# A decoder layer on one core: attention scores computed twice, small TensorE tiles, and a new order on every engine

## The reference

```
x = x + attention(layernorm(x))          # 16 heads of 16, causal, W_qkv, W_out
x = x + cross(layernorm(x), context)     # one head over 256 features, key mask
x = x + ffn(layernorm(x))                # 256 -> 2 x 704 -> 256
attention: softmax(Q K^T / 4 + causal) V for each head, then W_out
cross:     softmax(x ctx^T / 16 + mask) ctx
bit_linear(x, w, g): xn = rms_norm(x, g)
                     xq = round(xn * 127/max|xn|), an integer per row times a scale
                     wq = round(w / mean|w|) clipped to -1, 0, 1, times mean|w|
                     xq @ wq.T
ffn:       gate, up = bit_linear(x, gate_w, g1);  h = gate*sigmoid(gate)*up
           bit_linear(h, down_w, g2)
```

## Time and profile before

| | us |
|---|---|
| median of 3 runs (254.17 to 254.43) | 254.26 |
| profiled execution | 254.95 |
| its span, first to last instruction | 253.2 |
| TensorE busy, share of the span | 218.7, 86% |
| VectorE | 215.2, 85% |
| ScalarE | 147.9, 58% |
| GpSimd | 110.7, 44% |
| mean granted TensorE clock, of full | 0.922 |

### The profile page before, as it was taken

The page is one execution under the profiler, slowest core; times in us unless marked ns, Lnnn a source line. Parts: engine busy times, 40 slices in busy tenths (PEclk is TensorE's granted clock), DMA queues, the critical chain, the costliest instruction groups (busy, mean ns, idle before and its releaser), DMA issues. The chain is left out here.

```text
span 253.2 us, 7285 instructions
## 1 busy us (share of the span) xinstructions
PE 218.7 (86%) x2384; PEld 167.2 (66%) x2384; DVE 215.2 (85%) x639; ACT 147.9 (58%) x386; POOL 110.7 (44%) x209
## 2 busy tenths in 40 slices
PE   3867899989899999999999999999999999666433
PEld 3746686758686868686868686868687877442121
DVE  1398948699999999999999999999999989988741
ACT  2024273657685868585858585858585858443231
POOL 7222011337272727272726262727263626464640
PEclk9975999999999999999999999999999999975555
DMA  6993001010101010101010101001010111000000
GB/s 212 377 356 99 0 3 43 4 41 3 45 22 44 23 43 23 45 21 44 21 46 23 43 23 41 25 25 41 27 39 17 50 34 32 1 25 0 21 21 21
DMA packets 11108, 12.81 MB, mean 51 GB/s; under 512 B 1025, under 2 KB 10305, under 8 KB 11073
## 3 DMA queue, kind: packets, MB, share of 16 engines
q1 hardware_dynamic: 11008, 12.36, 15.0%
q0 software_dynamic: 64, 0.00, 0.0%
HBM read 10.26 MB, written 2.10 MB: 49 GB/s over the span
## 5 line engine op out<-in xcount | busy, mean ns | idle before, releaser
L1348 POOL TENSOR_TENSOR zh<-hh,gd 128x352 f32<-128x352 f32 x16 | 15.2, 947 | 54.4 <-DVE hh L1025 54.4
L320 PE MATMUL bankU<-yaT,wqkv 128*128 128x128 f32 x256 | 35.2, 295 | 0.8 <-ACT yaT L627 0.6
L320 PEld LDWEIGHTS bankU<-yaT,wqkv 128*128 128x128 f32 x256 | 32.7, 207 | 3.1 <-ACT yaT L627 1.6
L1324 POOL TENSOR_SCALAR ve<-mv 128x1 f32<-128x1 f32 x48 | 9.9, 206 | 50.5 <-DVE mv L867 30.2
L1326 POOL TENSOR_TENSOR rs<-ve,neghalf 128x1 f32<-128x1 f32 x48 | 26.6, 554 | 4.0
L304 PE MATMUL psS<-kz,qT 32*64 32x128 f32 x512 | 21.3, 280 | 0.0
L293 PE MATMUL bankG<-wg,zT 128*128 128x352 bf16 x64 | 15.9, 331 | 4.9 <-DVE hh L1025 3.6
L627 ACT ACTIVATE pT<-psS 128x512 f32<-128x512 f32 x32 | 19.1, 597 | 0.8
L1370 POOL TENSOR_SCALAR hq<-zh,qh 128x704 f32<-128x704 f32 x16 | 13.7, 858 | 10.7 <-issue 10.7
L332 PE MATMUL bankA<-wqkv,yaT 128*64 128x128 f32 x256 | 18.3, 288 | 0.0
L399 PE MATMUL bankB<-wo,oT 128*128 128x256 f32 x64 | 16.7, 384 | 1.7 <-ACT oT L627 1.6
(11 more groups left out here) (125 smaller groups left out, 584.7 us busy)
## 6 DMA issues: line engine op xcount, KB each, us to landing
ct_in<-ctx_t SPq DMA_DIRECT2D x16, 128.0 KB, 2.1
cn_in<-ctx_n SPq DMA_DIRECT2D x16, 128.0 KB, 2.3
out<-o_out SPq DMA_DIRECT2D x16, 128.0 KB, 1.7
wg<-gate_t SPq DMA_DIRECT2D x1, 1408.0 KB, 8.9
x_in<-x SPq DMA_DIRECT2D x1, 1280.0 KB, 11.6
wqkv<-wqkv_t SPq DMA_DIRECT2D x1, 768.0 KB, 6.0
wd<-down_t SPq DMA_DIRECT2D x1, 640.0 KB, 9.2
x_in<-x SPq DMA_DIRECT2D x1, 512.0 KB, 8.6
```

The costliest lines, as they stand in the source:

```text
L320: last = pe.matmul(qk_ps[:, e * P:(e + 1) * P], wqk[:, c, e * P:(e + 1) * P], yaT[:, c, :], start=(c == 0), stop=(c == DC - 1))
L1348: G.tensor_tensor(zh[:, 0:HALF], hh[:, 0:HALF], gd[:, 0:HALF], ALU.mult).then_inc(ev["zh_d0"], 1)
```

## The change

1. Scores are computed two times. `scores_q` has queries on partitions as before, but serves only for the maxima. `max_hi`, `max_rest`, `max_mid`, `max_lo` split each maximum into three bf16 numbers, `transpose_max` and `keep_max` bring them to partitions. `scores_k` computes scores with keys on partitions and adds minus the maximum by a product with a matrix of 0 and -1 (`less_bf`). The exponential reads that out of PSUM and writes `pT` directly. Both subtractions, eight transposes and two copies are gone.
2. Matmuls use smaller tiles: 32x64 in both scores (eight positions), 128x32 in `project_v` and `readout` (four). Twice the matmuls in the latter two.
3. `normalise_x` and `integers_h` go to GpSimd. The sums of weights go to ScalarE, the ternary down weights to GpSimd.
4. Each engine has one list for all tiles: a start, ten times a step body (s = 5 to 14), an end. Buffers are double by tile, context is four deep, `x1` is kept for all tiles. PSUM banks are assigned anew.
5. The mask matmul of the cross attention has 128 rows. Constants come as 8-bit and are converted on GpSimd; the load of wqkv is split in two.

```diff
-                    pe.matmul(psS[:, g, 0:256], ident_bf[:, :], causal_bf[:, :], start=True, stop=False)
...
+            def scores_q(t, *users):
...
+                for half in range(2):
+                    for g in range(4):
+                        rows = slice(32 * g, 32 * g + 32)
+                        for b in range(2):
+                            pe.matmul(psS[SEQ * b:SEQ * (b + 1), g, 0:256].rearrange("p (n k) -> p n k", k=SEQ), pick_bf[rows, half, :],
+                                      causal_bf[rows, half, :].unsqueeze(1).broadcast_to([32, 4, SEQ]),
+                                      start=(half == 0), stop=False)
+                for c in range(DC):
+                    for g in range(4):
...
+                            last = pe.matmul(psS[SEQ * b:SEQ * (b + 1), g, c * P:(c + 1) * P],
+                                             qT[rows, t % 2, c, SEQ * b:SEQ * (b + 1)],
+                                             kz[rows, t % 2, c, b, :, :], start=False, stop=(c == DC - 1))
...
+            def scores_k(t, *users):
...
+                for half in range(2):
+                    for g in range(4):
...
+                        for j in range(2):
+                            pe.matmul(psS[SEQ * j:SEQ * (j + 1), g, 256:512].rearrange("p (n q) -> p n q", q=SEQ)[:, :, 32 * half:32 * half + 32],
+                                      causal_bf[rows, half, :], ident_bf[rows, rows].unsqueeze(1).broadcast_to([32, 4, 32]),
+                                      start=(half == 0), stop=False)
+                for c in range(DC):
+                    for b in range(2):
+                        first = 256 + c * P + b * SEQ
+                        for g in range(4):
...
+                            for j in range(2):
+                                pe.matmul(psS[SEQ * j:SEQ * (j + 1), g, first:first + SEQ], kz[rows, t % 2, c, b, j, :],
+                                          qT[rows, t % 2, c, SEQ * b:SEQ * (b + 1)], start=False, stop=False)
+                for c in range(DC):
+                    for g in range(4):
...
+                        for j in range(2):
+                            last = pe.matmul(psS[SEQ * j:SEQ * (j + 1), g, 256 + c * P:256 + (c + 1) * P], less_bf[rows, 2 * c + j, :],
+                                             mT[rows, t % 2, :], start=False, stop=(c == DC - 1))
...
+                            for k in range(4):
+                                last = pe.matmul(o_ps[32 * k:32 * (k + 1), i, :, :], pT[:, t % 2, 2 * g + c, 32 * k:32 * (k + 1)],
+                                                 v2[:, t % 2, k // 2, i, :, :], start=True, stop=True)
...
+            def exponentials(t, half):
...
+                nc.scalar.activation(pT[:, t % 2, 4 * half:4 * half + 4, :].rearrange("p (g c) t -> p g (c t)", g=2),
+                                     psS[:, 2 * half:2 * half + 2, 256:512], ACT.Exp).then_inc(ev[f"exp_d{half}"], 1)
```

The step body on TensorE:

```diff
+            for s in range(5, 15):
+                transpose_yx(s - 2, ("v_d", s))
+                readout(s - 1, ("x1_d", s - 1))
+                gate_up_1(s - 4, ("mx_d", s + 1))
+                transpose_ya(s + 1, ("h1_d0", s - 3))
...
+                down(s - 5, ("h1_d1", s - 3))
+                transpose_max(s, ("hT_d1", s - 4))
+                project_out(s - 1, ("oT_d", s))
+                transpose_cross_weights(s - 2, ("yaT_d", s + 2))
+                scores_k(s, ("hh_d1", s - 3), ("expx_d", s - 1), ("mT_d", s + 1), ("out_d", s - 4))
+                cross_readout(s - 2, ("pxT_d", s - 1))
+                transpose_z(s - 3, ("q_d", s + 2), ("k0_d", s + 2), ("k1_d", s + 2))
+                project_v(s, ("hT_d0", s - 4))
+                scores_q(s + 1, ("exp_d0", s + 1), ("exp_d1", s + 1))
+                gate_up_0(s - 3, ("x2_d", s - 1), ("zT_d", s - 2))
```

More of the change, by code:

```diff
@@ L22 @@
 IC = -(-INTER // P)
+GW = 2 * INTER
 EPS = 1e-5
@@ L25, with decoder_kernel @@
 BIG = 2.0 ** 100
[L26 to L68, removed]
+C_ID, C_PARITY, C_ALL = 0, 128, 130
+B_PICK, B_CAUSAL, B_LESS, B_SEQ, B_ALL = 0, 128, 256, 512, 640
+TERMS = 8
 WARM = 7
-FILL_TO = 3
-LOOP_FROM, LOOP_TO = 5, 15
+CTX = 4
 def after(eng, sem, value):
-    if not isinstance(value, int) or value > 0:
+    if value > 0:
         eng.wait_ge(sem, value)
[L82 to L99, removed]
+def decoder_kernel(nc, x, ctx_n, ctx_t, mask, wqkv_t, wout_t, gate_t, down_t, g_gate, g_down, const, bits, out):
     T = x.shape[0]
-    GW = 2 * INTER
     with ExitStack() as stack:
@@ L228, in decoder_kernel, with freed @@
         ev = {n: sem(n) for n in names.split()}
+        ev["wmean_set"] = wmean_set
         block = stack.enter_context(nc.Block())
-        def run(eng, fill, step, drain, between={}):
-            for s in range(-1, LOOP_FROM):
-                (fill if s <= FILL_TO else step)(Step(s, 0, T, ev))
-                if s in between:
-                    between[s]()
-            for s in range(LOOP_FROM, T + 4):
-                (step if s < T else drain)(Step(s, 0, T, ev))
+        def freed(users):
+            for name, count in users:
+                nc.tensor.wait_ge(ev[name], count)
         @block.sync
@@ L300, in score_group @@
                 for c in range(DC):
-                    for g in (2 * half, 2 * half + 1):
+                    for g in range(4):
                         rows = slice(32 * g, 32 * g + 32)
@@ L620, in _ @@
-            pe.wait_ge(wqk_in, 16)
-            run(pe, fill, step, drain, {0: before_readout, 1: before_cross, 2: before_gate, 3: before_down})
+                pe.matmul(ps[:, 7, 0:P], ident, ident, start=True, stop=True)
+            pe.wait_ge(id_bf, 1)
+            transpose_ya(0)
+            project_v(0)
+            project_qk(0)
+            transpose_ya(1, ("yaT_d", 1))
+            scores_q(0)
+            project_qk(1, ("q_d", 1), ("k0_d", 1), ("k1_d", 1))
+            transpose_max(0, ("mx_d", 1))
@@ L850, in _ @@
             act.wait_ge(cst_in, 16)
-            run(act, fill, step, drain)
+            keep_yaT(0)
+            keep_k_1(0)
+            keep_q(0)
+            keep_yaT(1)
+            keep_k_0(0)
+            keep_v(0)
+            sum_gate()
+            keep_max(0)
+            keep_q(1)
+            keep_k_0(1)
+            keep_yaT(2)
+            exponentials_0(0)
+            exponentials_1(0)
+            keep_k_1(1)
+            sum_down()
+            keep_oT(0)
+            keep_max(1)
```

2214 lines of the change are left out of this document (1205 added, 1009 removed).

## The result

The changed kernel takes 259.27 us (258.48 to 262.14, 4 runs) against 254.21 for the kernel before on the same chip, a ratio of 1.022 (95% interval 1.014 to 1.030): slower, and clear of noise, though the interval leaves open whether by more than 2%. Forecast were 217 us, with 238 as the upper end.

The account below looks back on a forecast made before the run. VectorE was taken as the bound, TensorE 0.1 us behind. Fill 58.5, ten steps 111 and drain 46.8 make 216.3 us of span, 218.0 with what lies outside, 217.3 against the median; forecast 217 us, eight-in-ten range 204 to 238.

Parts of the forecast that it names:

- GpSimd gains 0.48 (as L1342, 256 values) and 0.86 (as L1370, 704): GpSimd per step: taking over x's normalisation and hq's conversion raises it from 6.42 to 7.8 us, hidden in the step.
- nothing in the gaps shows an engine out of instructions: TensorE's record starts in the old trace: argument that twice the records would not hold TensorE up.
- rival A: TensorE cannot keep up with twice the records, 0.027 us each: step 14 us, kernel 261 us; chance 0.12.
- D: Rival, TensorE's scores: only four small tiles run side by side, not eight; step 12.2, kernel 233 us; chance 0.08.
- The sign that I set for A: TensorE's small-tile groups: records coming at 0.025 us or more over a whole group would show the forecast wrong.
- TensorE needs 10.6: TensorE per tile in the loop: 12.3 us less 3.83 and 0.2, plus 2.34 added, gives 10.6 us.
- VectorE 9.95 busy, 10.6 with its idle time: VectorE per tile: 12.36 us less 2.84 and 0.21, plus 0.64, is 9.95; with idle and less overlap 10.6.
- rival C: GpSimd blocks VectorE twice a step: step 11.1 + 0.9 us, kernel 227 us; chance 0.08.
- 0.3 for such waits: Loop step: 0.3 us for VectorE and TensorE waiting on each other, part of the 11.1 us step.
- Rival B: The loop through the maxima, their split and both scores sets the step: 12 us, kernel 227 us; chance 0.2.
- Fill 58.5: Start of the kernel, before the ten steps: falls from 72.4 to 58.5 us, bounds 54 and 66.
- Drain 46.8: End of the kernel, after the ten steps: falls from 51.7 to 46.8 us, bounds 42 and 52.

Follow-up runs that it names:

- e2: The changed kernel with readout and project_v back in 64-column tiles: 252.36 us, 0.992 of the kernel before.
- f2: The changed kernel with integers_h and normalise_x in (mult, add) form on GpSimd, and readout and project_v in 64 columns: 246.87 us, 0.973 of the kernel before.
- g4: The changed kernel with 64-column readout and project_v, (mult, add) GpSimd forms, down weights on VectorE, x's tiles 2 to 5 earlier, VectorE's loop reordered: 232.45 us.
- g3: f2 with VectorE's loop reordered, residual_3 ahead of inner_largest and the operations splitting the maxima moved up: 241.46 us, 0.950 of the kernel before.
- f1: The changed kernel with only integers_h and normalise_x put in (mult, add) form on GpSimd: 253.40 us, 0.996 of the kernel before.
- h4: The kernel of g4 with integers_h and normalise_x back in the change's own (add) and (subtract, mult) forms on GpSimd: 243.30 us, 0.956 of the kernel before.
- h1: The kernel of g4 with the change's small tiles back, readout in 64 records and project_v in 32: 242.96 us.
- p1: The kernel before with eight forms of GpSimd operations added after its last result, each twice, a probe for durations: 270.52 us, one run.

## Why the prediction was wrong

Its picture of what was removed and added holds; what it said would hide the rest does not. Going from the changed kernel to the mended one, edit by edit: wide tiles 6.9 us (e2), cheap forms 5.5 (f2 against e2), x early 6.0, VectorE's order 5.4, down weights 2.8. That is 26.6 of the 28.4 between 259.27 and 230.92; the shares hang on the order of the edits, as the forms show (5.5 here, 12.4 when put back at the end). What is left to the forecast, 230.3 of span in g4 against 216.3, lies in all three stretches: 5.5 in the loop, 2.8 in the fill, 5.7 in the drain. The prediction's own sign of being wrong, a loop that ends after 180 us, came true at 203.0.

- **"GpSimd gains 0.48 (as L1342, 256 values) and 0.86 (as L1370, 704)", "still hidden": failed.** They took 1.23 and 1.99 us. The analogues agreed in size and type and not in the pair of operations. GpSimd's 9.7 us in a step are still less than the step, but `integers_h` ends behind the place where TensorE wants it. The bound from both sides that the prediction gave other unknown costs was not given here. It was also wrong that the conversion's longer time counts only in the drain; there it is on the chain too: the chain of waits at its end goes through three of them, at 232.8, 239.8 and 246.4.
- **"nothing in the gaps shows an engine out of instructions": failed**, and with it the ground for giving rival A 0.12. A's place was right, TensorE short because of twice the records, and its mechanism wrong. The pace that A feared does not exist: 32 records of the first scores start within 0.40 us, eight at once. Windows of L311 in the changed kernel (records under way):
```profile
139.23:139.27 0.04, 0.03 (x8) 0.04 (x16) 1.00 0.22 77
...
139.24:139.64 0.40, 0.40 (x32) 0.40 (x32) 1.00 0.06 18
```
  This settles D (false): sets of eight start 0.11 us apart. The sign that I set for A, records at 0.025 us or more over a whole group, did not come, and the kernel lost all the same. The small tiles of `readout` ran as forecast, 0.70 (127.14 to 127.84). The floor of about 25 ns in the Trainium skill, "TensorE: Matmul & The Clock Gate", section "Wait — 56ns, not 53.3ns?", does not hold from tile to tile here: starts stand 3 to 4 ns apart. What ran out was the supply of code, for which the page of before had a row (20 packets) that I did not read.
- **TensorE needs 10.6: mis-sized.** It needs 11.65 with wide tiles (g3), 0.36 less or 11.3 with narrow ones. Scores by key take 1.08 instead of 0.80 (134.92 to 136.00 in the changed kernel): the later of their 96 records no longer start by sets of eight but singly, on average 10 ns apart. The other 0.4 I have not divided further.
- **VectorE 9.95 busy, 10.6 with its idle time: mis-sized.** It is busy 10.65 us in one of the steps shown and 11.2 in the others. Three of the four parts of the maxima cost 0.14 to 0.17, as taken, but the fourth (L897, a cast) takes 0.80 in every step of the loop: it starts 0.17 us into GpSimd's L1440 and ends with it. That is rival C, once a step and not twice. It was read off the overlap and not tested by itself, and not every GpSimd instruction does it: the cast of L887 took 0.14 in the middle of an L1426 (75.32).
- **"0.3 for such waits": mis-sized.** Between f2 and g3 0.6 us a step came off (12.27 to 11.65), and TensorE's two waits in f2 sum to 0.73. Rival B was true, hidden behind the first two causes: the step is 12.27 where it said 12, and the ring it named, through the maxima and their parts, closes over `residual_3`'s late place, which it did not name.
- **Fill 58.5: failed.** 70.2 measured, 61.3 mended. "while SP is idle" and "nothing, up to 1 us" for the new order of loads missed that x's later tiles moved behind `maxima(0)`'s predecessor on VectorE: a wait in an engine's order, which I had asked of other steps and not of this one. The down weights took 11.0 us of GpSimd (5.38 and 4.10, and 1.54 for the one pass in the cheap form), not 4.6. Two of the sums there do not come out either: 4608 values at 0.00084 are 3.9, not 4.6, and 4352 at ScalarE's 0.60 for 512 are 5.1, not 3.9 (the two sums took 2.55 and 1.49 us, and 0.40 more to read them out).
- **Drain 46.8: failed.** 54.4, and 51.8 with cheap forms (f1). Why it is 52.5 in the mended kernel, with 0.8 more than before, was not tested.

The chances were misjudged too: 0.87 for faster leaned on the sum of busy times. Of the five causes only GpSimd's forms are a duration that was wrong; the supply of code and three places in an order (x's load, VectorE's loop, the down weights) are in no sum of durations.

## To carry to other kernels

When a change multiplies instructions, count them in blocks of 256 and ask how fast the densest block is worked off; here every block worked off in 3.25 us or less was followed by a stop, and slower ones where the packet was late. Price an instruction on GpSimd only by a row with the same pair of operations, and write an addition as (mult, add) with 1.0. And when an edit is undone and the time hardly moves, look at what waits in its place, wait by wait: the costly GpSimd forms seemed worth 5.9 us where the ring through VectorE stood behind them (f1), and were worth 12.4 once all else was mended (h4).

## What the runs showed of the hardware

- TensorE's code comes in packets of 16384 bytes, 256 instructions, one for each such border (38, 32 and 20 in three kernels). The next block starts 1.2 us or more after the end of its packet; stops of 0.4 to 2.0 us in the changed kernel, up to 2.9 in h1.
- GpSimd, one tensor-scalar instruction: 704 values 0.855 us (mult, add), 1.98 (add); 256 values 0.482 (mult, add), 0.864 (add), 1.23 (subtract, mult). A plain cast of 704 took 0.771 (all p1).
- Eight small tiles (32x64) start their matmuls 3 to 4 ns apart. In longer runs the pace falls: the 96 records of the scores by key start within 0.94 us, 10 ns apart on average, the 64 of `readout` within 0.57, 9 ns apart.
- A cast of 16 values on VectorE took 0.14 us alone (116.41), 0.80 beside GpSimd's L1440 and 3.77 beside L1510, each time up to the end of GpSimd's instruction, and 0.14 beside an L1426.
